# Row maximum as one rounded value, two steps' products together, reciprocals spread by four DMAs from SyncE: windowed attention and a ternary layer on one Trainium2 core

## The chip, the core and the metric

The kernel runs on one core of one Trainium2 chip. The time is device time in microseconds (us) from start to end of one execution. TensorE (PE) multiplies matrices, VectorE (DVE), ScalarE (ACT) and GpSimd (POOL) work element by element, SyncE (SP) issues most transfers between SBUF and DRAM. A median of three runs is given for the kernel before; the profile is of one execution of its own.

## The reference

`x` is 2048 tokens by 512, float32.

```python
qkv = layernorm(x) @ Wqkv                      # 512 -> 3 * 512
q, k = rope(rmsnorm(q, q_norm_w)), rope(rmsnorm(k, k_norm_w))   # 16 heads of 32
scores = q @ k.T / sqrt(32)                    # token i sees i-255 .. i
x = x + (softmax(scores) @ v) @ Wo
w_q = ternary(weight, 0.2, 0.6) + rram_variation
x = x + ternary(layernorm(x), 0.33, 0.5) @ w_q.T
```

## The kernel before, in words

**Three stages.** Up to about 188 us the inputs are normalised, projected, rotated and split: a float32 value is kept as a high part in TensorE's rounded form (float32r) and a low part, so that products of the three pieces high/high, high/low and low/high come near to float32. The pieces of q and k go to `qk_scr` in DRAM (L310). From about 188 to 463 us attention runs head by head. Then come the output projection (L703) and the ternary layer (L731).

**Attention** has 16 heads of 8 steps, `STEPS` = 128. A step has two tiles of 128 queries. All engines walk the same step numbers, each in a program of its own:

- TensorE, `scores` (L593), for step s: queries against three tiles of keys, into one of two pairs of PSUM banks. The left operand is a slice of `q_stack`, 128 rows: 96 of the three pieces, and 32 below them. Rows 96 and 97 of `q_stack` hold zeros at this time, and rows 96 and 97 of `k_stack` ones; the rest is zeros.
- VectorE, `merge` (L1169) and `maximum` (L1183): the largest masked score of each query, negated, in `neg_max`. `scores` of step s waits for the maximum of step s-2.
- After each fourth step `split_maxima` (L1192, L1194) splits eight columns of `neg_max` into high and low, TensorE transposes them to 16 rows (L601), VectorE copies them out (L1201), and SyncE writes them by DMA into rows 96 and 97 of `q_stack` (L418). This is step `M_TR` = 4c + 5 for half head c.
- TensorE, `scores_t` (L622), ten steps later (`ST_LAG`): the transposed scores S^T of the same step, keys against queries. The rows 96 and 97 now subtract the maximum. Its target `BANK_ST + e` is one bank for each of the two tiles; the tile's next S^T waits until ScalarE has read it (`expd`).
- ScalarE, `exponentials` (L849), two for each step, into `prob`; GpSimd zeroes what the window excludes (L1010, L1014).
- TensorE, `times_v` (L658): a half of the products of probabilities with `v` and with ones at each step, in 32-column tiles of the array. Each float32 matmul there shows as two in the trace.
- ScalarE copies results to `o_stage` (L859), SyncE stores them to `o_t` and the sums to `sum_scr` (L443, L447).

**Reciprocals.** A unit u is half of the tokens of four heads; there are eight. When its sums are in DRAM, they are loaded (`sums`), inverted on VectorE (L1237), stored (`rec_scr`), and spread over the 32 rows of each head into `rec_bc`; VectorE then divides `o_t` (L1244), two operations a unit. `after` gives the step at which a unit is complete. The tables `LOAD_SUMS`, `RECIP`, `STORE_RECS`, `SPREAD` and `DIVIDE` give the step of each. For u = 0 to 5 ScalarE issues the three transfers (L875, L881, L889), for the last two SyncE (L393, L399, L407). Steps go on to `LAST` = 160.

**SyncE's program** does at step s, in this order: the maxima's rows, the loads of the stacks of later heads (L368, at s % 8 of 6 and 2), staged results, spreads. A wait there holds all that stands behind it.

## Time and profile before

| | us |
|---|---|
| median of 3 runs | 561.16 (555.36 to 561.59) |
| the profiled execution | 562.22 |
| its span, first to last instruction | 560.3 |
| TensorE busy | 477.7 (85%) |
| VectorE busy | 382.6 (68%) |
| ScalarE busy | 212.1 (38%) |
| GpSimd busy | 226.4 (40%) |
| mean granted TensorE clock | 0.939 of 2.4 GHz |

Busy time is the time in which an engine had an instruction under way. Matmuls are pipelined and their ends are modelled, so a busy TensorE is not one at its peak. The chain of work that ended last is followed back from the end: 47% of the span on it is TensorE, 23% are transfers, 13% VectorE. The span less the busy time of an engine says nothing about where that engine was waited for.

### The profile page before, as it was taken

The page shows a single profiled execution, that of the slowest core. Times are in us where ns is not written, and L with a number is a line of the kernel's source. Part 1 is how long each engine was busy: PE and PEld are TensorE (multiplying, and loading weights), DVE is VectorE, ACT ScalarE, POOL GpSimd, SP SyncE. Part 2 cuts the span into 40 slices and gives each one's busy share as a digit, 9 for nine tenths or more (in the row PEclk, how much of TensorE's full clock was granted, in tenths as well). Part 3 has the DMA queues.
Part 4 walks back from the last instruction along what each step waited for, and adds up shares of the span by engine and source line. Part 5 has one row for each costly group of instructions (what it writes and reads, how often), then busy time and mean ns, then how long its engine had stood idle before and what let it go on. Part 6 is the DMA issues. An engine that isn't in the chain of part 4 may idle for free.

```text
span 560.3 us, 10469 instructions
## 1 busy us (share of the span) xinstructions
PE 477.7 (85%) x3648; PEld 338.8 (60%) x3648; DVE 382.6 (68%) x808; ACT 212.1 (38%) x464; POOL 226.4 (40%) x351
## 2 busy tenths in 40 slices
PE   1897997997997518797997799988997998788997
PEld 1685886786885305454664466555664656666775
DVE  3798478578377718484885888776775710798994
ACT  2451332233133114353554355534554471322121
POOL 2175288288297013242443244333443372423000
PEclk9998999999999858798999799988999799798999
DMA  8520466553548569766566455654454104302433
GB/s 289 202 77 0 168 207 227 176 173 143 187 152 216 199 181 235 256 170 159 142 179 165 117 168 142 183 150 113 138 143 122 50 23 127 99 23 75 135 110 132
DMA packets 42776, 83.41 MB, mean 149 GB/s; under 512 B 6803, under 2 KB 13747, under 8 KB 42471
## 3 DMA queue, kind: packets, MB, share of 16 engines
q1 hardware_dynamic: 40205, 79.40, 46.5%
q10 hardware_dynamic: 2520, 3.34, 2.1%
q8 instruction: 30, 0.49, 0.4%
q14 instruction: 21, 0.17, 0.1%
HBM read 48.12 MB, written 30.15 MB: 140 GB/s over the span
## 4 chain that ended last, share of the span: by engine, by line
PE 47%; DMA 23%; DVE 13%; POOL 6%; issue 5%; SPq 3%; ACT 2%; DVEq 0%; ACTq 0%; POOLq 0%
PE psum L658 12%; PE psum L622 9%; DMA rec_bc<-rec_scr 8%; DMA region_w<-max_rows 6%; PE psum L525 6%; PE psum L593 5%; PE psum L731 5%; PE psum L511 4%; PE psum L703 3%; DMA rec_scr<-recs 2%; SPq L310 2%; DMA qk_scr<-region_t 2%; POOL normed L983 2%; DVE region_o L1076 2%; DMA region_m<-in_x 2%
## 5 line engine op out<-in xcount | busy, mean ns | idle before, releaser
L849 ACT ACTIVATE region_m<-psum 128x384 f32<-128x384 f32 (+2 forms) x256 | 106.5, 468 | 134.9 <-PE psum L622 122.5
L1010 POOL TENSOR_SCALAR_AFFINE_SELECT region_m<-region_m 128x256 f32<-128x256 f32 x128 | 52.1, 407 | 167.0 <-ACT region_m L849 166.7
L658 PE MATMUL psum<-region_m,v 128*32 128x128 f32 (+1 forms) x992 | 113.8, 339 | 0.0
L658 PE MATMUL psum<-region_m,ones 128*32 128x128 f32 (+1 forms) x992 | 113.7, 338 | 0.0
L593 PE MATMUL psum<-region_w 128*128 128x384 f32 (+2 forms) x256 | 70.8, 362 | 29.4 <-DMA region_w<-qk_scr 15.7
L511 PE MATMUL psum<-region_t,region_w 128*128 128x512 f32 x384 | 93.6, 401 | 1.4 <-ACT region_t L763 1.4
L1169 DVE COPY_PREDICATED psum<-mask,psum 128x256 f32<-128x256 uint32 x128 | 54.5, 425 | 54.3 <-PE psum L593 38.9
L622 PE MATMUL psum<-region_w 128*128 128x384 f32 (+2 forms) x256 | 80.5, 397 | 12.7 <-DMA region_w<-max_rows 11.5
L511 PEld LDWEIGHTS psum<-region_t,region_w 128*128 128x128 f32 x384 | 72.5, 191 | 18.1 <-ACT region_t L763 1.8
L1183 DVE TENSOR_REDUCE neg_max<-psum 128x2 f32<-128x512 f32 x112 | 76.6, 684 | 2.5
L658 PEld LDWEIGHTS psum<-region_m,v 128*32 128x32 f32 x992 | 52.0, 112 | 42.6 <-issue 25.7
L622 PEld LDWEIGHTS psum<-region_w 128*128 128x128 f32 x256 | 40.9, 198 | 54.5 <-issue 41.2
L593 PEld LDWEIGHTS psum<-region_w 128*128 128x128 f32 x256 | 49.0, 207 | 33.3 <-DMA region_w<-qk_scr 14.1
L1076 DVE SCALAR_TENSOR_TENSOR region_o<-psum,qkw,region_m 128x512 f32<-128x512 f32 x64 | 43.6, 742 | 29.7 <-ACT region_o L774 29.7
L703 PE MATMUL psum<-region_t,region_w 128*128 128x512 f32 x192 | 48.5, 408 | 5.4 <-DVE region_w L1283 5.4
L658 PEld LDWEIGHTS psum<-region_m,ones 128*32 128x32 f32 x992 | 52.0, 112 | 0.0
L525 PE MATMUL psum<-region_w,region_t 128*128 128x512 f32 x192 | 49.2, 412 | 0.0
L703 PEld LDWEIGHTS psum<-region_t,region_w 128*128 128x128 f32 x192 | 37.8, 198 | 14.3 <-ACT region_w L868 5.8
L1014 POOL TENSOR_SCALAR_AFFINE_SELECT region_m<-region_m 128x256 f32<-128x256 f32 x112 | 45.5, 406 | 0.0
L525 PEld LDWEIGHTS psum<-region_w,region_t 128*128 128x128 f32 x192 | 36.8, 193 | 10.2 <-issue 2.7
L731 PE MATMUL psum<-region_t,region_w 128*128 128x512 f32 x128 | 34.5, 415 | 4.7 <-DVE normed L1325 4.7
L983 POOL TENSOR_TENSOR normed<-normed,half_h 128x512 fp32r<-128x512 f32 x26 | 33.5, 1312 | 11.6 <-ACT half_h L795 11.6
(88 smaller groups left out, 548.0 us busy)
## 6 DMA issues: line engine op xcount, KB each, us to landing
region_w<-qk_scr SPq DMA_DIRECT2D x60, 384.0 KB, 4.9
qk_scr<-half_h SPq DMA_DIRECT2D x56, 256.0 KB
region_m<-in_x SPq DMA_DIRECT2D x32, 256.0 KB, 3.4
qk_scr<-normed SPq DMA_DIRECT2D x28, 256.0 KB
region_o<-normed SPq DMA_DIRECT2D x64, 64.0 KB
out<-normed SPq DMA_DIRECT2D x16, 256.0 KB, 2.0
rec_bc<-rec_scr ACTq DMA_DIRECT2D x6, 512.0 KB
qk_scr<-region_t SPq DMA_DIRECT2D x8, 256.0 KB
```

The costliest lines, as they stand in the source:

```text
L511: last = nc.tensor.matmul(psum[:, BANK_PAIR + 2 * (n % 2) + half, :], w, x_t[g % 2][:, b, k, :], start=(k == 0 and a + b == 0), stop=(k == ...
L525: last = nc.tensor.matmul(psum[:, BANK_PAIR + 2 * (n % 2) + e, :], x_t[g % 2][:, b, k, P * i:P * (i + 1)], wv[:, a, k, :], start=(j == 0), ...
L593: last = nc.tensor.matmul(psum[:, 2 * (n % 2) + e, P * (k0 - qt + 2):3 * P], qs[:, P * qt:P * (qt + 1)], ks[:, P * k0:P * (qt + 1)], start ...
L622: last = nc.tensor.matmul(psum[:, BANK_ST + e, 0:P * (q1 - kt)], ks[:, P * kt:P * (kt + 1)], qs[:, P * kt:P * q1], start=True, stop=True)
L658: last = nc.tensor.matmul(psum[32 * r:32 * r + 32, BANK_O + c % 2, at:at + P * width], w, probs, start=start, stop=stop, tile_position=(0, ...
L703: last = nc.tensor.matmul(psum[:, BANK_WO + t % NWO, :], o_split[g % 2][:, a, c, P * i:P * (i + 1)], wo[:, b, c, :], start=(c == 0 and a + ...
L731: last = nc.tensor.matmul(psum[:, BANK_FFN + t % 2, :], xq_t[t % 2][:, c, :], wf[:, a, c, :], start=(j == 0), stop=(j == 7))
L849: nc.scalar.activation(prob[:, n % NPT, e, 0:cols], psum[:, BANK_ST + e, 0:cols], ACT.Exp, scale=SCALE).then_inc(expd, 1)
L1010: nc.gpsimd.affine_select(out=near, in_=near, compare_op=ALU.is_ge, fill=0.0, base=0, pattern=[[0, 2], [1, P]], channel_multiplier=-1).the ...
L1076: vec.scalar_tensor_tensor(rope[:, i, :], psum[:, banks + half, :], qkw[:, 2 * p + half:2 * p + half + 1], trig[:, g % 2, s, :], ALU.mult, ...
L1169: vec.copy_predicated(psum[:, 2 * (n % 2):2 * (n % 2) + 2, 0:P], mask[:, :, :].bitcast(U32), psum[:, 2 * (n % 2):2 * (n % 2) + 2, 2 * P:3 ...
L1183: vec.tensor_reduce(neg_max[:, h % 2, 2 * j:2 * j + 2], psum[:, slot:slot + 2, 0:2 * P], axis=AX_X, op=ALU.max, negate=True).then_inc(maxe ...
```

## The change

**Row maximum.** `tensor_reduce` now writes `neg_max` in float32r, so the value is rounded once, and the transpose takes it as it is: no `split_maxima`, 8 rows instead of 16, one row of the stack (96) instead of two. A rounded maximum is as good a shift as an exact one, since numerator and sum use the same.

**No zero rows.** `scores` contracts over 96 rows and `scores_t` over 97. The 32 rows of zeros and ones, their staging in DRAM, their loads for three stacks and the zeroing of two rows for each later head are gone; what is left is one row of ones for each of three stacks.

**Products of two steps together**, and another order of S^T and scores in every second step.

**Reciprocals.** All transfers of all units are issued by SyncE; one DMA for each head spreads 32 rows; the steps of the tables are earlier for units 0 to 5.

```diff
-        LOAD_SUMS = {n + (3 if u in BY_ACT else 2): u for u, n in after.items()}
-        RECIP = {n + (6 if u in BY_ACT else 5 + 2 * (u % 2)): u for u, n in after.items()}
-        STORE_RECS = {n + (8 if u in BY_ACT else 5 + 2 * (u % 2)): u for u, n in after.items()}
-        SPREAD = {n + (10 if u in BY_ACT else 7 + 2 * (u % 2)): u for u, n in after.items()}
-        DIVIDE = {n + (14 if u in BY_ACT else 10 + 3 * (u % 2)) + 2 * q: 2 * u + q
-                  for u, n in after.items() for q in range(2)}
+        LOAD_SUMS = {n + 3 - u % 2: u for u, n in after.items()}
+        RECIP = {n + 5 - u % 2: u for u, n in after.items()}
+        STORE_RECS = {n + 6 - u % 2: u for u, n in after.items()}
+        SPREAD = {n + 8 - u % 2: u for u, n in after.items()}
+        DIVIDE = {n + 11 - u % 2 + 2 * q: 2 * u + q for u, n in after.items() for q in range(2)}
...
-            eng.wait_ge(zero_set, 1)
-            rest = P - STACKED
-            eng.dma_start(zero_scr, rec_bc[0:rest, :]).then_inc(a_zero, 16)
-            eng.dma_start(ones_scr[MAXROWS:rest, :], rec_bc[0:rest - MAXROWS, :]).then_inc(a_zero, 16)
             eng.wait_ge(const_set, 4)
...
-                eng.dma_start(f32(q_stack[i][STACKED:P, :]), zero_scr).then_inc(a_ones[i], 16)
-                eng.dma_start(f32(k_stack[i][STACKED:P, :]), ones_scr).then_inc(a_ones[i], 16)
+                eng.dma_start(f32(k_stack[i][STACKED:STACKED + 1, :]), ones_scr).then_inc(a_ones[i], 16)
...
-                    eng.dma_start(f32(q_stack[i][STACKED:STACKED + MAXROWS, cols]),
-                                                        zero_scr[0:MAXROWS, cols]).then_inc(a_zeros[i][half], 16)
...
+                if s in LOAD_SUMS:
...
+                if s in STORE_RECS:
...
+                if s in SPREAD:
+                    u = SPREAD[s]
+                    c, half = divmod(u, 2)
+                    eng.wait_ge(a_recs[half], 16 * (c + 1))
+                    if c:
+                        eng.wait_ge(o_done, 2 * (u - 2) + 2)
+                    for h in range(4):
+                        eng.dma_start(
+                            rec_bc[HEAD_DIM * h:HEAD_DIM * (h + 1), 1024 * half:1024 * (half + 1)],
+                            rec_scr[half, 4 * c + h:4 * c + h + 1, :].to_broadcast(
+                                [HEAD_DIM, SEQ // 2])).then_inc(a_bc[half], 16)
...
             for s in range(STEPS + PV_LAG + 1):
-                if 0 <= s - ST_LAG < STEPS:
+                n = s - PV_LAG
+                if n % 2 and 0 <= s - ST_LAG < STEPS:
                     scores_t(s - ST_LAG)
                 if s < STEPS:
                     scores(s)
...
-                n = s - PV_LAG
-                if n > 0:
-                    times_v(n - 1 + n % 2, 1 - n % 2)
+                if n % 2 == 0 and 0 <= s - ST_LAG < STEPS:
+                    scores_t(s - ST_LAG)
+                if n > 0 and n % 2 == 0:
+                    for part in range(2):
+                        times_v(n - 1, part)
```

**TensorE in a quiet part of attention**, before. L622 is S^T, L593 the scores, L658 one half of the products; `x2` means two such instructions in a row.

```order
L622 MATMUL psum<-region_w 128x384 x2
L593 MATMUL psum<-region_w 128x384 x2
L658 MATMUL psum<-region_m,v 32x256
L658 MATMUL psum<-region_m,ones 32x256
L658 MATMUL psum<-region_m,v 32x256
L658 MATMUL psum<-region_m,ones 32x256
L658 MATMUL psum<-region_m,v 32x128
L658 MATMUL psum<-region_m,ones 32x128
L658 MATMUL psum<-region_m,v 32x128
L658 MATMUL psum<-region_m,ones 32x128
L622 MATMUL psum<-region_w 128x384 x2
```

And the same place now (L602 is S^T, L572 the scores, L638 the products):

```order
L602 MATMUL psum<-region_w 128x384 x2
L572 MATMUL psum<-region_w 128x384 x4
L602 MATMUL psum<-region_w 128x384 x2
L638 MATMUL psum<-region_m,v 32x256
L638 MATMUL psum<-region_m,ones 32x256
L638 MATMUL psum<-region_m,v 32x256
L638 MATMUL psum<-region_m,ones 32x256
L638 MATMUL psum<-region_m,v 32x128
L638 MATMUL psum<-region_m,ones 32x128
L638 MATMUL psum<-region_m,v 32x128
L638 MATMUL psum<-region_m,ones 32x128
```

The scores of two steps now stand in one run between two S^T, and both halves of the products (sixteen rows, of which eight are shown) follow the second S^T.

**SyncE around the first unit**, steps 45 to 49, before. L418 writes the maxima's rows, L368 loads a stack, L443 and L447 store staged results; the transfers of the reciprocals stand in ScalarE's program.

```order
L418 DMA region_w<-max_rows 2x8x128
L365 DMA region_w<-zero_scr 2x1024
L368 DMA region_w<-qk_scr 96x1024 x2
L443 DMA sum_scr<-normed 2x2x256
L447 DMA region_o<-normed 32x2x256 x2
L418 DMA region_w<-max_rows 2x8x128
```

And now, the same steps (L380, L354, L405, L409 for the same transfers; L422 stores reciprocals, L416 loads the next unit's sums, L431 spreads):

```order
L380 DMA region_w<-max_rows 1x8x128
L354 DMA region_w<-qk_scr 96x1024 x2
L422 DMA rec_scr<-recs 128x32
L405 DMA sum_scr<-normed 2x2x256
L409 DMA region_o<-normed 32x2x256 x2
L416 DMA sums<-sum_scr 128x32
L431 DMA rec_bc<-rec_scr 32x1024 x4
L380 DMA region_w<-max_rows 1x8x128
```

Between the rows of step 45 and those of step 49 there are now one store, one load and four spreads more, and one zeroing less.

## Rows read from the trace of the kernel before

**Rows 1.** Stretches, matmuls of L622 alone: length, PE, PEld busy (count), PEclk, DMA share, GB/s.

```profile
260.00:290.00 30.00, 10.60 (x36) 5.36 (x36) 1.00 0.53 145
290.00:322.00 32.00, 8.46 (x28) 4.32 (x28) 0.89 0.57 152
352.00:388.00 36.00, 10.43 (x32) 5.26 (x32) 0.91 0.58 157
418.00:443.00 25.00, 7.38 (x22) 3.69 (x22) 0.86 0.35 95
```

**Rows 2.** The chain of waits near 290 us: start, length, what.

```profile
290.27 3.99 DMA rec_scr<-recs
294.28 14.47 DMA rec_bc<-rec_scr
```

**Rows 3.** Stretches of 2 us, all engines; the last two columns are DMA share, GB/s.

```profile
194.00:196.00 2.00, 0.00 (x0) 0.00 (x0) 2.00 (x6) 0.08 (x1) 0.00 (x0) 0.50 0.52 203
474.00:476.00 2.00, 0.00 (x0) 0.00 (x0) 0.00 (x0) 0.00 (x0) 0.00 (x0) 1.00 0.26 99
```

**Rows 4.** The timeline of one step: start, length, engine, line, what, idle before.

```profile
286.16 0.44 PE L622 MATMUL psum<-region_w 128*128 128x384 f32 x1
286.44 0.33 PE L622 MATMUL psum<-region_w 128*128 128x384 f32 x1
286.61 0.34 PE L593 MATMUL psum<-region_w 128*128 128x384 f32 x1
286.70 0.87 ACT L849 ACTIVATE region_m<-psum 128x384 f32<-128x384 f32 x2 [0.92 <-PE psum L622]
287.05 0.40 PE L658 MATMUL psum<-region_m,v 128*32 128x256 f32 x1
287.16 0.43 DVE L1169 COPY_PREDICATED psum<-mask,psum 128x256 f32<-128x256 uint32 x1 [0.21 <-PE psum L593]
287.62 0.69 DVE L1183 TENSOR_REDUCE neg_max<-psum 128x2 f32<-128x512 f32 x1
287.84 0.62 PE L622 MATMUL psum<-region_w 128*128 128x384 f32 x2
```

**Rows 5.** Timeline and chain after the last scores, where steps have S^T and products only.

```profile
452.84 0.62 PE L622 MATMUL psum<-region_w 128*128 128x384 f32 x2
454.18 0.62 PE L622 MATMUL psum<-region_w 128*128 128x384 f32 x2
461.44 2.13 PE psum L658 x48
```

**Rows 6.** The chain before and in the first heads, and a stretch as in rows 3.

```profile
192.17 10.82 DMA qk_scr<-region_t
219.43 10.87 DMA region_w<-max_rows
218.00:230.00 12.00, 8.31 (x98) 4.79 (x96) 6.97 (x18) 4.55 (x11) 3.47 (x9) 0.96 0.87 237
```

**Rows 7.** The chain at the end of attention.

```profile
466.65 1.68 DMA rec_scr<-recs
468.35 8.79 DMA rec_bc<-rec_scr
479.37 1.63 PE psum L703 x3
```

**Rows 8.** The timeline of SyncE in step 46 and of TensorE at the end of attention.

```profile
288.86 1.82 SPq L368 DMA_DIRECT2D region_w<-qk_scr  x2
479.37 9.06 PE L703 MATMUL psum<-region_t,region_w 128*128 128x512 f32 x27 [5.42 <-DVE region_w L1283]
```

**Rows 9.** The timeline of VectorE at the second group of inputs.

```profile
21.21 2.47 DVE L1042 BATCH_NORM_STATS2 stats<-region_m 128x6 f32<-128x512 f32 x4 [2.53 <-DMA region_m<-in_x]
```

**Rows 10.** Groups by line and shape: busy us, mean ns, idle before.

```profile
L1228 DVE TENSOR_SCALAR region_t<-psum 128x128 fp32r<-128x128 f32 x16 | 4.5, 282 | 0.0
```

**Rows 11.** The tile `rec_scr`, all its eight stores.

```profile
DMA to landing us min/median/max: 1.4/4.7/9.4
```

More of the change, by code:

```diff
@@ L43 @@
 STACKED = 3 * HEAD_DIM
-MAXROWS = 2
 NSTACK = 3
@@ L143, in build @@
         NWO = 5
-        zero_set, a_zero = steps("zero_set"), steps("a_zero")
+        a_one = steps("a_one")
         const_set, mask_set, ident_cast = steps("const_set"), steps("mask_set"), steps("ident_cast")
@@ L165, in build @@
         a_ones = [steps(f"a_ones{i}") for i in range(NSTACK)]
-        a_zeros = [[steps(f"a_zeros{i}{half}") for half in range(2)] for i in range(NSTACK)]
         a_rows = [steps(f"a_rows{i}") for i in range(2)]
@@ L447, in _ @@
                         eng.dma_start(dst[:, e], src).then_inc(a_stage[c % 2], 16)
-                if s in SPREAD and SPREAD[s] not in BY_ACT:
-                    spread_recs(SPREAD[s])
-                if s in LOAD_SUMS and LOAD_SUMS[s] not in BY_ACT:
-                    load_sums(LOAD_SUMS[s])
-                if s in STORE_RECS and STORE_RECS[s] not in BY_ACT:
-                    store_recs(STORE_RECS[s])
+                if s in LOAD_SUMS:
+                    u = LOAD_SUMS[s]
+                    c, half = divmod(u, 2)
+                    eng.wait_ge(a_stage[half], 48 * (4 * c + 4))
+                    if u - 2 >= 0:
+                        eng.wait_ge(recd, u - 1)
+                    eng.dma_start(sums[:, u % 2, :], sum_scr[half, 4 * c:4 * c + 4, :].rearrange(
+                        "h (i t) -> (h i) t", t=32)).then_inc(a_sums[u % 2], 16)
+                if s in STORE_RECS:
+                    u = STORE_RECS[s]
+                    c, half = divmod(u, 2)
+                    eng.wait_ge(recd, u + 1)
+                    eng.dma_start(rec_scr[half, 4 * c:4 * c + 4, :].rearrange("h (i t) -> (h i) t", t=32),
+                                  recs[:, half, :]).then_inc(a_recs[half], 16)
+                if s in SPREAD:
+                    u = SPREAD[s]
+                    c, half = divmod(u, 2)
+                    eng.wait_ge(a_recs[half], 16 * (c + 1))
[6 more added lines that the diff above has]
+                                [HEAD_DIM, SEQ // 2])).then_inc(a_bc[half], 16)
                 if s in (STEPS + PV_LAG + 2, STEPS + PV_LAG + 4):
@@ L593, in scores @@
                     last = nc.tensor.matmul(psum[:, 2 * (n % 2) + e, P * (k0 - qt + 2):3 * P],
-                                            qs[:, P * qt:P * (qt + 1)],
-                                            ks[:, P * k0:P * (qt + 1)], start=True, stop=True)
+                                            qs[0:STACKED, P * qt:P * (qt + 1)],
+                                            ks[0:STACKED, P * k0:P * (qt + 1)], start=True, stop=True)
                 last.then_inc(score, 1)
             def maxima_to_rows(c, s):
-                eng.wait_ge(m_low, c + 1)
-                nc.tensor.transpose(psum[0:2 * PAIRS, 2 * (s % 2), 3 * P:4 * P],
-                                              f32(max_split[:, c % 2, :]), ident[:, :]).then_inc(m_tr, 1)
+                h, half = divmod(c, 2)
+                eng.wait_ge(maxed, 4 * c + 4)
+                nc.tensor.transpose(psum[0:PAIRS, 2 * (s % 2), 3 * P:4 * P],
+                                    f32(neg_max[:, h % 2, PAIRS * half:PAIRS * (half + 1)]), ident[:, :]).then_inc(m_tr, 1)
             def transpose_w(i):
@@ L947, in _ @@
             nc.gpsimd.memset(mask[:, :, :], 1.0).then_inc(const_set, 1)
-            nc.gpsimd.memset(rec_bc[:, :], 0.0).then_inc(zero_set, 1)
             eng.wait_ge(const_set, 4)
@@ L1023, in _ @@
                     for half in range(2):
-                        eng.wait_ge(a_bc[half], 16 * CHUNKS)
+                        eng.wait_ge(a_bc[half], 64 * CHUNKS)
                     for i in (2, 3):
@@ L1175, in maximum @@
                 eng.wait_ge(merged, n + 1)
-                if h >= 2:
-                    eng.wait_ge(m_low, 2 * (h - 2) + j // 4 + 1)
+                if h >= 2 and j % 4 == 0:
+                    eng.wait_ge(m_tr, 2 * (h - 2) + j // 4 + 1)
                 if j == 0:
```

90 lines of the change are left out of this document (12 added, 78 removed).

## The prediction

> **What bounds the kernel now.** I read the page's totals, then the matmuls of one line counted stretch by stretch, then the chain of waits at the places where the count falls, then single steps. The totals are a mean over stages that have different limits, so nothing below rests on them. The profiled execution took 562.2 us, 0.2% over the median of 561.2; the sum below is made against 562.2. The change touches attention (about 188 to 479 us) and little else.
>
> In attention every step issues two matmuls of L622, so their count gives the pace. 260 to 290 us has 36 of them: 18 steps, 1.667 us each; two more stretches of 30 us (322 to 352, 388 to 418) have 36 too. The three between them, in which reciprocals are spread, have 28, 32 and 22, that is 14, 16 and 11 steps, which should take 23.3, 26.7 and 18.3 us and take 32, 36 and 25 [rows 1]. They lose 8.7 + 9.3 + 6.7 = 24.7 us, part of it at the half clock (granted 0.89, 0.91 and 0.86 against 1.00).
>
> The chain of waits names the loser: `rec_bc<-rec_scr` takes 14.47 us from issue to landing [rows 2], and VectorE, which has the division next in its program, can't go on to the maxima. On an idle core it takes 8.79 us too [rows 7]. Why so long: while it is alone in flight, the share of the DMA engines is 0.26 at 99 GB/s, four engines of sixteen at 25 GB/s; the `qk_scr` stores, whose outermost size is 8, show 0.52 at 203 GB/s [rows 3]. The old access pattern has 4 heads outermost. The Trainium skill, DMA: Bandwidth & Descriptors, in "Why a DMA increments its semaphore by 16 and not by 1", says that a DMA uses the largest count up to 16 that divides the outermost sizes of both sides: 4 before, 16 for a new piece of 32 rows; the trace agrees as far as it goes (0.26 and 0.52).
>
> **The spread: engines.** A new piece is 128 KB over 32 rows. 
> **The spread: order.** The cover changes, since sums, reciprocals and spreads now stand in SyncE's one program and queue, and DIVIDE comes 11 steps after the units' table entry `after` instead of 14. First unit: SyncE issues the stack load of step 46 at 288.86 for 1.82 us [rows 8]; the store of the reciprocals goes behind it, 290.7; it takes 3.99 as before [rows 2], 294.7; four spreads are issued until 297.1 and land by 299.1. VectorE comes to the division of step 51 at 296.6 (step 46 starts at 286.16 [rows 4], five steps of 1.667, and 2.15 until the maximum ends). It waits 2.5 us. TensorE feels it only at scores two steps on, about 1 us. Meanwhile the row maxima of step 49, behind the spreads in SyncE's program, go out at 297.1 instead of 293.4 and land at 299.2; S^T of step 53 wants them at 298.3: 0.9, mostly the same wait. I take 1.5 us for a unit, 3 for a stretch of two, 9 for all three; no half clock. Gain 24.7 − 9 = **15.7 us** (bounds 0 and 24.7). ScalarE no longer stands in these waits, which TensorE felt little.
>
> **Zero rows.** Four fills of 256 KB go before the last stores, and two in front of the third stack. The last store is issued at 192.17 and lands 10.82 us later [rows 6], with eight engines full at 25.4 GB/s each [rows 3]; 1 MB over 16 engines is 65.5 KB on each of them: **2.6 us** less before the loads that TensorE waits for. The row maxima issued at 219.43 wait 10.87 us behind a backlog that moves 237 GB/s [rows 6]; 0.5 MB less is **2.1 us** (bounds 0 and 4.7 for both). At the start 0.5 MB goes from before `load_x(1)`, for which VectorE idles 2.53 us [rows 9]; its next consumer, the squares, waits for matmuls until 25 us anyway: 0.4 (0 to 1.3). The small zero loads of each head are 8 KB: nothing. The contraction goes from 128 rows to 96 and 97; no row here has fewer than 128. The spacing of 0.17 us is 0.01 over the 384 columns at 2.4 GHz, so 512 matmuls could give 5 us at most; I take 0.
>
> **Row maximum.** The two small VectorE operations for each half head go, 64 in all; VectorE is not what TensorE waits for in a quiet stretch, so 0. The transpose waits for `maxed` 4c+4, which the scores ahead of it have waited for already.
>
> **Products together.** Two steps were S^T, S, PV, S^T, S, PV; now S^T, S, S, S^T, PV, PV. From the row times [rows 4]: the first S^T matmul starts at 0, the second at 0.28, the scores at 0.45, the product at 0.89, the next S^T at 1.68. Within one kind the spacing is 0.17, so a junction costs about 0.11 before S^T's second matmul, 0.10 between scores and product, and 0.12 after products (48 matmul pieces, three parts, in 2.13 against 3 × 0.79 [rows 5]). A pair of steps saves 0.33 of 3.36. But the bank of S^T is single: the second S^T waits for the exponentials of the first. They start 0.54 after it and end at 1.41 [rows 4]. In the new order the second matmul of the second S^T would load at 1.13; it must wait until 1.45. That gives back 0.32: **0 us** for 59 pairs (bounds: −19.5 without that wait; +3.5 if the release of the bank takes 0.1 and not 0.04). VectorE now gets two scores 0.34 apart. Its merge starts 0.55 after the scores and merge and maximum take 1.15 [rows 4], so the later maximum ends at 3.35; the scores that want it start at 3.35 + 0.79 = 4.14. The slack of 0.8 holds a division (0.7) but not the splitting of a ternary weight (four operations of 0.28 [rows 10]): 8 × 0.3 = **+2.4**. After step 128 there are no scores to stand between two S^T: the second S^T starts 1.18 after the first (the first exponential ends at 0.97, release 0.04, load 0.17), its second matmul at 1.62, products at 1.89 for 1.46: 3.35 against 2 × 1.34 [rows 5]; 5 pairs, **+3.3**.
>
> **The tail.** TensorE idles 5.42 us before L703, to 479.37 [rows 8], on the last spread but one (468.35, 8.79) [rows 7]. In the new program the store of its reciprocals goes after two x loads (about 0.9 after the 466.65 of before), lands beside them about 470, the pieces are out at 472.5 and land at 474.5: **−2.7**, and **−0.8** for the half clock after the idle (three matmuls in 1.63 us [rows 7], half of that at the full one). Bounds −1 and −6. The last unit comes 10 us earlier, but its division on GpSimd is hidden before and after.
>
> Sum: 562.2 − 15.7 − 4.7 − 0.4 + 2.4 + 3.3 − 3.5 = **543.6 us**.
>
> **Rivals.**
> (a) *S^T does not wait*: the exponentials start earlier than I read, and the junctions count in full, 59 × 0.33 = 19.5: 524 us. For it: TensorE is fully busy in quiet stretches, no exponential being waited for. Against: the 1.41 is a row. Chance 0.15.
> (b) *Four pieces are no faster*: they read the same rows again and again, and a spread still lands 8.8 us after its issue, now later by 1.8 and with SyncE behind it. The stretches keep their 24.7: 562.2 − 4.7 − 0.4 + 5.7 − 1 = 562 us. The Trainium skill, DMA: Bandwidth & Descriptors, "Rules for kernel authors", says of transfers to disjoint partition halves "Don't bother — they serialize", and wants one of 128 partitions; that holds for pieces that already use all engines, which the 0.26 says this one does not. Chance 0.12.
> (c) *Stalls of 3 us for each unit* because VectorE has lost its slack: 9 more: 553 us. Chance 0.12.
> (d) *SyncE holds the row maxima* (the slower side): in its program they stand behind the wait for the reciprocals' landing. It decides when a unit costs more than 4.1 us (24.7 / 6). With the longest landing of reciprocals, 9.4 us [rows 11], instead of 3.99, the row maxima go out at 302.5 and come 6 us late for S^T, and the half clock after it costs 1.7 (0.11 of 32 us, for two units [rows 1]): 7.7 × 6 = 46, less the 9 that I have, is 37 over my sum, 581 us. For it: a stack load is ahead in the same queue. Against: 3.99 was measured beside the same load. Chance 0.05.
> The forecast, 535 to 552 us, has 0.56.
>
> **Numbers.** 543.6 us is that of the likeliest. With (a) and (c) inside, 524 to 555 leaves (b), (d) and a little out: 8 in 10. A difference of 2% is what a measurement can tell here, so faster means under 549.9: forecast almost whole (0.50), (a) 0.15, and a part of (c) 0.04: 0.69. Within 2%: 0.24, mostly (b) and (c). Slower: 0.07, (d) and what I don't see.
>
> **What would show it.** Landing of `rec_bc` pieces within 5 us of the first issue, and a share near 1 while they fly; the three stretches at 1.8 us a step with a granted clock near 1; TensorE's S^T waiting for ScalarE's exponentials some 0.3 us in each pair (about 18 us in the table of waits), else (a); VectorE waiting for `rec_bc` under 10 us instead of 24.6 in sum; the idle before the first last-chunk projection near 3 us; the first row-maximum waits shorter. Wrong it would be if the queue of SyncE makes reciprocals land late.

## The result, and the profile after

The changed kernel takes **540.1 us** (median of 4 runs, 536.9 to 546.0) against 560.7 us of the kernel before (4 runs, 555.4 to 561.6) on the same chip: a ratio of 0.963, 95% interval 0.955 to 0.972. The forecast was 543.6 us in a range of 524 to 555. Some executions of every kernel take some per cent longer at a lower granted clock: medians are of all runs, and ratios compare the others alone. The changed kernel's profiled execution took 536.9 us with a span of 534.1; the one of before, 562.2 with a span of 560.3. The two traces so differ by 26.2 us where the medians differ by 20.6: the profiled execution after is the quickest of its kernel's runs, and the one before lies 1.5 us above its median.

I cut both traces at the same work: the issue of the row maxima of the seventh half head (257.8 before, 250.2 after), that of the last half head (451.4 and 421.4), the last product of attention (463.5 and 436.5), and the restart of TensorE in the output projection (479.4 and 450.7).

| stretch | before | after | change | forecast |
|---|---|---|---|---|
| to the seventh row maxima | 257.8 | 250.2 | −7.6 | −5.1 |
| 100 steps to the last row maxima | 193.6 | 171.2 | −22.4 | −13.3 |
| to the last product | 12.1 | 15.1 | +3.0 | +3.3 |
| to the projection's restart | 15.9 | 14.2 | −1.7 | −2.7 |
| to the end | 80.9 | 83.4 | +2.5 | −0.8 |

The matmuls of S^T (now L602) by stretches, which answer to [rows 1]: start and end, length, PE, PEld busy (count), PEclk, DMA share, GB/s.

```profile
258.00:288.00 30.00, 11.10 (x36) 5.88 (x36) 1.00 0.61 172
288.00:318.00 30.00, 9.85 (x34) 5.43 (x34) 1.00 0.66 179
318.00:348.00 30.00, 10.16 (x32) 5.66 (x33) 0.94 0.61 164
380.00:410.00 30.00, 10.80 (x34) 5.59 (x34) 1.00 0.51 142
```

A stretch with spreads now holds 32 to 36 matmuls in 30 us, where there were 28 in 32 and 22 in 25, and the clock is nearly whole. In the 100 steps TensorE was at its half clock for 22.5 us before and for 3.4 after.

The DMA issues of SyncE in the after trace, one unit of reciprocals (start, length, queue, line, what), then the page's row for all 32 pieces (KB each, median us to landing), then who waited (total, times, longest).

```profile
283.31 1.71 SPq L431 DMA_DIRECT2D rec_bc<-rec_scr  x4
285.07 0.72 SPq L380 DMA_DIRECT2D region_w<-max_rows  x1
```

```profile
rec_bc<-rec_scr SPq DMA_DIRECT2D x32, 128.0 KB, 2.7
```

```profile
DVE region_o L1185 <- DMA rec_bc<-rec_scr: 8.7, 5, 2.7
PE psum L602 <- ACT region_m L832: 7.4, 7, 4.1
PE psum L602 <- DMA region_w<-max_rows: 3.3, 4, 1.5
```

One wait is new. SyncE's program waits for the landing of the reciprocals' store before it issues the spreads, and the next row maxima stand behind them. The wait in the whole run (total, times, longest), and two pieces of the chain of waits near 340 us (start, length, what):

```profile
SPq L431 <- DMA rec_scr<-recs: 6.4, 7, 2.3
```

```profile
334.12 5.10 DMA rec_scr<-recs
341.00 2.25 DMA region_w<-max_rows
```

Here SyncE issues nothing from 338.1 to 339.24, then the four spreads, then the row maxima, and S^T starts when these have landed.

The four pieces of this unit are issued within 1.7 us and the last lands at 287.3, 4.0 us after the first issue, for 14.47 in [rows 2]; each piece posts 16 semaphore updates when it lands, where the old DMA posted 5. VectorE waits 8.7 us for reciprocals in all, for 24.6 before.

### The profile page after: what moved, and what is told of

The parts are those of the page before. It is cut to its first block, busy times and chain, and to the rows that moved or that the text cites. A ratio compares the mean times of both kernels' runs of the same rounds, so it can differ in the third digit from the quotient of the medians.

```text
span 534.1 us, 10283 instructions
## 1 busy us (share of the span) xinstructions
PE 465.0 (87%) x3648; PEld 345.1 (65%) x3648; DVE 369.4 (69%) x744; ACT 210.5 (39%) x464; POOL 226.3 (42%) x350
## 4 chain that ended last, share of the span: by engine, by line
PE 49%; DVE 17%; DMA 10%; SPq 8%; issue 7%; POOL 4%; ACT 3%; DVEq 0%; ACTq 0%; POOLq 0%
PE psum L638 11%; PE psum L602 8%; PE psum L506 8%; PE psum L492 5%; PE psum L714 5%; PE psum L572 5%; PE psum L686 4%; DMA rec_scr<-recs 3%; DVE region_o L1028 3%; SPq L409 2%; DMA region_w<-max_rows 2%; DMA rec_bc<-rec_scr 2%; PE psum L527 2%; DVE diag L1040 2%; SPq L354 1%
## 5 line engine op out<-in xcount | busy, mean ns | idle before, releaser
L962 POOL TENSOR_SCALAR_AFFINE_SELECT region_m<-region_m 128x256 f32<-128x256 f32 x128 | 54.3, 424 | 141.4 <-ACT region_m L832 141.4
L638 PE MATMUL psum<-region_m,ones 128*32 128x128 f32 (+1 forms) x992 | 98.9, 330 | 0.0
L638 PE MATMUL psum<-region_m,v 128*32 128x128 f32 (+1 forms) x992 | 98.9, 330 | 0.0
L602 PE MATMUL psum<-region_w 97*128 97x384 f32 (+2 forms) x256 | 81.7, 394 | 10.6 <-ACT region_m L832 7.4
L572 PE MATMUL psum<-region_w 96*128 96x384 f32 (+2 forms) x256 | 66.4, 367 | 19.9 <-DMA region_w<-qk_scr 13.3
L1135 DVE TENSOR_REDUCE neg_max<-psum 128x2 fp32r<-128x512 f32 x112 | 76.6, 684 | 2.5
L602 PEld LDWEIGHTS psum<-region_w 97*128 97x128 f32 x256 | 44.0, 196 | 50.2 <-issue 33.6
L638 PEld LDWEIGHTS psum<-region_m,v 128*32 128x32 f32 x992 | 57.8, 111 | 20.7 <-issue 7.8
L572 PEld LDWEIGHTS psum<-region_w 96*128 96x128 f32 x256 | 45.7, 203 | 29.3 <-DVE neg_max L1135 13.1
L638 PEld LDWEIGHTS psum<-region_m,ones 128*32 128x32 f32 x992 | 57.8, 111 | 0.0
L966 POOL TENSOR_SCALAR_AFFINE_SELECT region_m<-region_m 128x256 f32<-128x256 f32 x112 | 45.9, 409 | 0.0
```

Source lines behind the costliest of these rows:

```text
L572: last = nc.tensor.matmul(psum[:, 2 * (n % 2) + e, P * (k0 - qt + 2):3 * P], qs[0:STACKED, P * qt:P * (qt + 1)], ks[0:STACKED, P * k0:P * ...
L602: last = nc.tensor.matmul(psum[:, BANK_ST + e, 0:P * (q1 - kt)], ks[0:STACKED + 1, P * kt:P * (kt + 1)], qs[0:STACKED + 1, P * kt:P * q1], ...
L638: last = nc.tensor.matmul(psum[32 * r:32 * r + 32, BANK_O + c % 2, at:at + P * width], w, probs, start=start, stop=stop, tile_position=(0, ...
L962: nc.gpsimd.affine_select(out=near, in_=near, compare_op=ALU.is_ge, fill=0.0, base=0, pattern=[[0, 2], [1, P]], channel_multiplier=-1).the ...
L1135: vec.tensor_reduce(neg_max[:, h % 2, 2 * j:2 * j + 2], psum[:, slot:slot + 2, 0:2 * P], axis=AX_X, op=ALU.max, negate=True).then_inc(maxe ...
```

## The experiments

Times are medians, with the ratio to the kernel before on the same chip and its 95% interval.

**1. One spread for each unit.**

```diff
-                    for h in range(4):
-                        eng.dma_start(
-                            rec_bc[HEAD_DIM * h:HEAD_DIM * (h + 1), 1024 * half:1024 * (half + 1)],
-                            rec_scr[half, 4 * c + h:4 * c + h + 1, :].to_broadcast(
-                                [HEAD_DIM, SEQ // 2])).then_inc(a_bc[half], 16)
+                    eng.dma_start(
+                        rec_bc[:, 1024 * half:1024 * (half + 1)],
+                        rec_scr[half, 4 * c:4 * c + 4, :].rearrange("h (o t) -> h o t", o=1).to_broadcast(
+                            [4, HEAD_DIM, SEQ // 2])).then_inc(a_bc[half], 16)
```

(In this kernel and the next the two waits on `a_bc` count 16 and 32 for a unit.)

> The changed kernel with the reciprocals of a unit spread by one DMA instead of four (same queue, same steps, same bytes). Theory E (DMA engines): one DMA over four heads is carried by few of the 16 engines, as in the kernel before, so it lands 9 to 14 us after its issue instead of 4, the divisions wait for it, the VectorE queue holds the row maxima behind them, and most of the 18 us that the stretches with spreads gained is lost: 552 to 560 us, with waits of VectorE for rec_bc of over 20 us in sum. Rival P (place): what helped is that SyncE issues the chain and issues it earlier; then the time stays at 538 to 543 us.

Measured: **574.1 us**, 1.020 (1.010 to 1.030). Theory E has the direction and is short by 14 us at least: this is slower than the kernel before. The profiled executions here (581.0 us) and in experiment 7 (569.5) are above their medians, so sums of waits read in them may be a few us too large.

**2. Two spreads of two heads.**

```diff
-                    for h in range(4):
+                    for h in (0, 2):
                         eng.dma_start(
-                            rec_bc[HEAD_DIM * h:HEAD_DIM * (h + 1), 1024 * half:1024 * (half + 1)],
-                            rec_scr[half, 4 * c + h:4 * c + h + 1, :].to_broadcast(
-                                [HEAD_DIM, SEQ // 2])).then_inc(a_bc[half], 16)
+                            rec_bc[HEAD_DIM * h:HEAD_DIM * (h + 2), 1024 * half:1024 * (half + 1)],
+                            rec_scr[half, 4 * c + h:4 * c + h + 2, :].rearrange("h (o t) -> h o t", o=1).to_broadcast(
+                                [2, HEAD_DIM, SEQ // 2])).then_inc(a_bc[half], 16)
```

> The changed kernel with a unit's reciprocals spread by two DMAs of two heads each. Theory E: the outermost dimension of a DMA (2 here) sets how many engines carry it, so each is carried by 2 of the 16 and both land no sooner than the single DMA of four heads does: 555 to 570 us, landing 9 to 18 us after the first issue. Rival N (number of pieces): more DMAs in flight are quicker whatever their shape; then it lies between the changed kernel and the one with a single spread, about 546 us.

Measured: **614.0 us**, 1.095 (1.087 to 1.102), slower by 40 us than with one spread and 44 above the range expected: theory E has the direction again, and what one more slow DMA costs it had far too low. The number of pieces is not what helps; each piece's shape is. Stretches of 1.5 and 4 us in which no engine works and a spread is what the DMA engines carry (PE, PEld, DVE, ACT, POOL busy, PEclk, DMA share, GB/s), first of experiment 1:

```profile
299.50:301.00 1.50, 0.00 (x0) 0.00 (x0) 0.00 (x0) 0.00 (x0) 0.00 (x0) 0.50 0.25 72
```

and of experiment 2:

```profile
301.00:305.00 4.00, 0.00 (x0) 0.00 (x0) 0.00 (x0) 0.00 (x0) 0.00 (x0) 0.50 0.13 52
```

A DMA of four heads keeps a quarter of the 16 DMA engines busy, one of two heads an eighth, and both sorts post that number of semaphore updates and one more (5 and 3). In experiment 2 the first piece's last two updates come at 300.15 and 301.01 and those of the second, issued 0.6 us behind it, at 305.14 and 306.00, 4.99 us after each; the share is 0.12 (299 to 300) while both are in flight. So they stand on the same two engines, one behind the other. The Trainium skill, DMA: Bandwidth & Descriptors, in "Why a DMA increments its semaphore by 16 and not by 1", says that a DMA issued from SyncE or ScalarE runs on the lowest-numbered engines. The trace does not number them; that both pieces share their two agrees.

**3. TensorE's order of before in the changed kernel.**

```diff
-                n = s - PV_LAG
-                if n % 2 and 0 <= s - ST_LAG < STEPS:
+                if 0 <= s - ST_LAG < STEPS:
                     scores_t(s - ST_LAG)
...
-                if n % 2 == 0 and 0 <= s - ST_LAG < STEPS:
-                    scores_t(s - ST_LAG)
-                if n > 0 and n % 2 == 0:
-                    for part in range(2):
-                        times_v(n - 1, part)
+                n = s - PV_LAG
+                if n > 0:
+                    times_v(n - 1 + n % 2, 1 - n % 2)
```

> The changed kernel with TensorE's order of before: S^T first in every step, one half of the products in every step. My account from the traces: a quiet pair of steps 3.28 -> 3.36 us (+4 us over some 50 pairs), the end phase behind the last score 3.1 us shorter, so 541 us (538 to 544). Rival: putting the products of two steps together is worth its nominal 0.3 us in each of 59 pairs; then 555 to 558 us.

Measured: **540.2 us**, 0.961 (0.952 to 0.969), inside the range expected: the products together are worth nothing as a whole that the medians can tell. By the trace the 100 steps take 177.3 us for 171.2 (with 7.6 us at the half clock for 3.4), and the stretch from the last row maxima to the last product 12.1 for 15.1; the rest of the difference lies ahead of attention's steady part, where kernels with the same front differ by up to 9 us in my traces (247.6 to 256.9 at the seventh row maxima).

**4. Four spreads in the kernel before.** The edit is that of experiment 1 backwards, in both functions `spread_recs`, with 64 for 16 in the waits on `a_bc`.

```diff
-                eng.dma_start(
-                    rec_bc[:, 1024 * half:1024 * (half + 1)],
-                    rec_scr[half, 4 * c:4 * c + 4, :].rearrange("h (o t) -> h o t", o=1).to_broadcast(
-                        [4, HEAD_DIM, SEQ // 2])).then_inc(a_bc[u % 2], 16)
+                for h in range(4):
+                    eng.dma_start(
+                        rec_bc[HEAD_DIM * h:HEAD_DIM * (h + 1), 1024 * half:1024 * (half + 1)],
+                        rec_scr[half, 4 * c + h:4 * c + h + 1, :].to_broadcast(
+                            [HEAD_DIM, SEQ // 2])).then_inc(a_bc[u % 2], 16)
```

> The kernel before with only the spread cut into four DMAs, of one head each, still issued by ScalarE at its old steps. Theory E: they land 4 us after the first issue, the 18 us in the stretches with spreads come back less the time that ScalarE takes to issue three more (its exponentials stand behind them, 3 x 0.4 us in each of 6 units, hidden or not): 543 to 550 us. Rival P: the place counts; then 556 to 561 us.

Measured: **545.5 us**, 0.975 (0.966 to 0.984), 14 us from this edit alone (9 to 19 by the interval), inside the range expected; the 100 steps take 175.8 us for 193.6. Which engine issues the chain, and at which step, shows no gain beside it: with SyncE's places, TensorE's old order and no zero rows (experiment 3) they take 177.3, one trace each.

**5. The row maximum and the zero rows, alone and apart.** Two kernels: the kernel before with the hunks of the diff on `MAXROWS`, `zero_scr`, `neg_max`, `max_split` and the row counts of the matmuls; and the same with the split into two values kept.

```diff
-                eng.dma_start(f32(q_stack[i][STACKED:P, :]), zero_scr).then_inc(a_ones[i], 16)
-                eng.dma_start(f32(k_stack[i][STACKED:P, :]), ones_scr).then_inc(a_ones[i], 16)
+                eng.dma_start(f32(k_stack[i][STACKED:STACKED + MAXROWS, :]), ones_scr).then_inc(a_ones[i], 16)
...
-                    eng.dma_start(f32(q_stack[i][STACKED:STACKED + MAXROWS, cols]),
-                                                        zero_scr[0:MAXROWS, cols]).then_inc(a_zeros[i][half], 16)
```

Expected of the first:

> The kernel before with only the row maxima changed: one value in TensorE's rounded form, 97 rows in S^T, no rows of zeros, ones written once; spreads and the order of TensorE as before. My account (front): the row-maximum DMA of the seventh half head is issued 7.6 us earlier in the changed kernel, nearly all of it from these parts, and the steps gain 1 to 3 us more because the row-maximum DMA now takes twice as many DMA engines and VectorE has no splitting: 548 to 553 us against 559. Rival: the front gain is a matter of the runs' start (the load of x); then 555 to 559 us.

Of the second:

> The kernel before with the rows of zeros and the fills for them gone, but the row maximum still split into two values (98 rows in S^T). The prediction put 4.7 us on the zero rows and nothing on the row maximum; the run with both came out 9.2 us faster. If the zero rows carry it all: 549 to 553 us. If the split and its two-row DMA were worth about half: 554 to 557 us.

Measured: the first **0.984** (0.978 to 0.989), about 551 us for 560.4 by the ratio (the median of all ten runs is 556.6); the second 553.7 us, **0.983** (0.974 to 0.992). The zero rows carry it all, 9 us (6 to 12 by the narrower interval), and the single row maximum nothing that can be told. In the trace of the second the seventh row maxima go out at 250.0 us (257.8 before) and the 100 steps take 191.9 for 193.6. A single trace is not enough for the first of these: the seventh row maxima go out at 257.7 to 262.9 us in the three traces of kernels with zero rows and at 247.6 to 256.9 in the eleven without, 6.8 us apart in the mean. The row maxima's DMA runs on four times the DMA engines and not on twice: it posts 9 updates for 3.

**6. Exponentials over 128 columns, after and before.** The same edit in both kernels.

```diff
-                    nc.scalar.activation(prob[:, n % NPT, e, 0:cols], psum[:, BANK_ST + e, 0:cols],
+                    nc.scalar.activation(prob[:, n % NPT, e, 0:P], psum[:, BANK_ST + e, 0:P],
```

> The changed kernel with each exponential over 128 columns instead of up to 384: two thirds of the exponentials' work is left out, so the output is not the reference's. Theory B (bank): in a quiet pair of steps the second S^T waits for the first exponentials to free its bank, and this is what held the pair at 3.28 us where its instructions need 3.03; then the pair falls to 3.0 to 3.1 us and the 100 steps between the seventh and the last row-maximum DMA take 158 to 163 us instead of 171. Rival I (issue): TensorE is bound by its own weight loads and issue; the pair stays at 3.25 to 3.3 us and the 100 steps at 168 to 172.

> The control: the kernel before with the same shorter exponentials (their other columns left out of the work). There S^T opens every step and waits for nothing in quiet steps, so by both theories its quiet pair stays at 3.36 us and its 100 steps at 188 to 196 us.

Measured, one run each: 528.5 us in the changed kernel, 563.8 in the one before. A quiet pair is two steps in which TensorE waits for no row maxima and no maximum. One in the timeline of TensorE (start, length, line, what), of the changed kernel:

```profile
268.41 0.61 PE L602 MATMUL psum<-region_w 97*128 97x384 f32 x2
268.86 0.98 PE L572 MATMUL psum<-region_w 96*128 96x384 f32 x4
269.67 0.64 PE L602 MATMUL psum<-region_w 97*128 97x384 f32 x2
271.68 0.61 PE L602 MATMUL psum<-region_w 97*128 97x384 f32 x2
```

its exponentials:

```profile
268.94 0.87 ACT L832 ACTIVATE region_m<-psum 128x384 f32<-128x384 f32 x2 [1.35 <-PE psum L602]
270.11 0.88 ACT L832 ACTIVATE region_m<-psum 128x384 f32<-128x384 f32 x2 [0.29 <-PE psum L602]
```

and with short exponentials, TensorE and then ScalarE:

```profile
267.25 0.62 PE L602 MATMUL psum<-region_w 97*128 97x384 f32 x2
267.71 0.86 PE L572 MATMUL psum<-region_w 96*128 96x384 f32 x4
268.41 0.51 PE L602 MATMUL psum<-region_w 97*128 97x384 f32 x2
270.29 0.62 PE L602 MATMUL psum<-region_w 97*128 97x384 f32 x2
```

```profile
267.79 0.45 ACT L832 ACTIVATE region_m<-psum 128x128 f32<-128x128 f32 x2 [1.42 <-PE psum L602]
```

The second S^T starts 1.26 us after the first beside whole exponentials and 1.16 beside short ones, its two matmuls are 0.64 and 0.51 us long, and the pair takes 3.27 and 3.04 us. Of the 55 pairs behind the first eight, the lower quarter goes from 3.26 to 3.03 us and the median from 3.28 to 3.23; what holds the other half near 3.2 stays open. In the kernel before the lower quarter stays at 3.37 and the 100 steps take 188.4, as expected. Theory B holds for the quiet pair and is too large for the whole: the 100 steps fall to 165.8 us, not to 158 to 163.

**7. One spread, with the divisions three steps later.** Why is experiment 1 slower than the kernel before, which has the same DMA? On top of its edit:

```diff
-        DIVIDE = {n + 11 - u % 2 + 2 * q: 2 * u + q for u, n in after.items() for q in range(2)}
+        DIVIDE = {n + (14 if u < 6 else 11) - u % 2 + 2 * q: 2 * u + q for u, n in after.items() for q in range(2)}
```

> The single spread per unit again, with the divisions of the first six units three steps later (14 steps behind the unit's end instead of 11). If the cost of the slow spread is that VectorE waits for it in its queue with the row maxima behind, six steps (9.7 us at 1.62 us each) between issue and division cover nearly all of a landing of 9 to 11 us: 541 to 548 us, against 574 with the early divisions. Rival: the long transfer itself disturbs (DMA engines, row-maximum DMAs, clock) wherever the division stands; then 555 us or more.

Measured: **566.6 us**, 1.004 (0.999 to 1.009). The rival is right in the main. In the steps VectorE no longer waits for `rec_bc` (29.3 us in experiment 1), and that gave only 7.5 us by the medians (574.1 to 566.6). The chain of waits of this kernel (start, length, what):

```profile
294.02 0.61 SPq L430
294.63 0.04 issue
294.67 9.04 DMA region_w<-max_rows
303.71 0.04 issue
303.76 1.01 PE psum L601 x2
```

The row maxima, 4 KB, are issued behind the spread and land at 303.71; the spread has landed at 303.53. This is a second path from the slow spread to TensorE, past VectorE: the maxima of this kernel take 9.0, 9.5 and 9.1 us behind the three first spreads, those of experiment 1 11.1, 9.2 and 10.3, those of experiment 2 14.1, 13.8 and 15.0, and 1.8 to 2.5 in the steps where no spread is ahead. Their updates show the place: of the eight that come with the landing, four of experiment 1 come 2.0 us after the issue (292.39 to 292.47) and four behind the spread's four (301.25 to 301.49 behind 301.07 to 301.31); in experiment 2 six come by 293.9 and two at 305.3 and 306.2, behind 305.1 and 306.0. Only what shares the spread's DMA engines is late. In the steps S^T waits for them three times, 19.4 us in sum here and 22.5 in experiment 1. In the kernel before it is there too, across queues: ScalarE's spread of [rows 2] lands at 308.75, and the maxima that SyncE issued at 300.71 land at 308.78. There, though, the spread was ten steps behind its unit and met the row maxima late in its flight; on SyncE, two steps earlier, they go out 0.65 us behind it and wait for nearly all of it.

**8. Both ends mended.** From step 128 on the old order of TensorE, and the loads of `x` behind the last spreads.

```diff
                 n = s - PV_LAG
-                if n % 2 and 0 <= s - ST_LAG < STEPS:
+                paired = s < STEPS
+                if (n % 2 or not paired) and 0 <= s - ST_LAG < STEPS:
...
+                if not paired:
+                    times_v(n - 1 + n % 2, 1 - n % 2)
...
-                if s in (STEPS + PV_LAG + 2, STEPS + PV_LAG + 4):
+                if s in (STEPS + PV_LAG + 6, STEPS + PV_LAG + 10):
```

> The changed kernel with two things mended at the end: behind the last score (step 128 on) TensorE goes back to S^T first and half the products in each step, and SyncE issues the four loads of x behind the stores and spreads of the last reciprocals instead of ahead of them. By the comparison of the traces the first gives 3.1 us (5.8 by the run of the alternating order) and the second 3 us on the chain from the last staging to the projection: 532 to 536 us against 540 of the changed kernel. Rival: the loads of x then come late for the first residual additions and the second gives nothing: 535 to 538 us.

Measured: **531.6 us** (6 runs, 525.8 to 537.5), 0.946 (0.941 to 0.951): faster than both kernels, and 0.4 us below the range expected. From the last row maxima to the last product it takes 12.1 us for 15.1, from there to the projection's restart 11.2 for 14.2. The chain at that place, first of the changed kernel:

```profile
440.15 3.88 DMA rec_scr<-recs
444.05 0.33 SPq L431
```

and of this one, where the store (issued at 433.39) lands in 2.10 us, before SyncE has issued what the last half head wants, and the chain goes by the spread:

```profile
437.07 2.77 DMA rec_bc<-rec_scr
439.84 0.02 issue
439.87 0.70 DVE region_o L1188
```

**9. Short subtractions on GpSimd, on top of 8.** What makes the stretch behind the restart longer than before?

```diff
+                n = GROUP if g == 0 else 32
-                nc.gpsimd.tensor_tensor(o_split[g % 2][:, 1, c, :], o_t[:, c, GROUP * g:GROUP * (g + 1)],
+                nc.gpsimd.tensor_tensor(o_split[g % 2][:, 1, c, 0:n], o_t[:, c, GROUP * g:GROUP * g + n],
```

> The version with both ends mended, and the late subtractions of GpSimd (the low halves of the output's splits, all but those of the first four hundred and more tokens) over 32 columns instead of 512; the rest of these halves is left out. Theory: VectorE's tensor_scalar over 128x512 takes 1.15 and 1.40 us beside these subtractions and 0.56 and 0.43 us alone; with them short all four such operations of the first two tiles fall to 0.4 to 0.7 us and the stretch from the projection's restart to the end from 82.0 to 79 to 80.5 us. Rival: these operations are slow for a reason of their own (first use, the half clock); then they keep their 1.1 to 1.4 us.

Measured, one run: 530.1 us. VectorE and then GpSimd in the changed kernel:

```profile
455.57 0.55 DVE L1250 TENSOR_SCALAR v<-v,mean_var,rstd 128x512 f32<-128x512 f32 x1
456.15 1.40 DVE L1253 TENSOR_SCALAR v<-v 128x512 bf16<-128x512 f32 x1
457.58 1.66 DVE L1257 SCALAR_TENSOR_TENSOR v<-v 128x512 bf16<-128x512 f32 x1
459.16 0.68 DVE L1234 TENSOR_TENSOR v<-psum,region_m 128x512 f32<-128x512 f32 x1
```

```profile
455.86 4.52 POOL L952 TENSOR_TENSOR region_w<-region_o,region_w 128x512 fp32r<-128x512 f32 x3 [4.13 <-ACT region_w L851]
```

In experiment 8 the same two TENSOR_SCALAR of the first tile take 1.15 and 1.40 us and the first of the second 1.17; here

```profile
454.21 0.63 DVE L1254 TENSOR_SCALAR v<-v,mean_var,rstd 128x512 f32<-128x512 f32 x1
454.88 0.49 DVE L1257 TENSOR_SCALAR v<-v 128x512 bf16<-128x512 f32 x1
455.40 1.66 DVE L1261 SCALAR_TENSOR_TENSOR v<-v 128x512 bf16<-128x512 f32 x1
```

with the last of them still beside GpSimd's multiplication (455.04 to 458.2). From the projection's restart to the end it is 78.4 us, for 82.0 in experiment 8: a little more than the 1.5 to 3 us expected. VectorE is busy for 62.8 us of it for 66.6, and 3.4 us of it are at the half clock for 6.8, which one run cannot take apart. The Trainium skill, SBUF — State Buffer, "SBUF: two separate sides", has VectorE and GpSimd share a pair of ports, which one of them holds for a whole instruction where VectorE's has two inputs in SBUF or runs in a mode that takes both its ports. The 1.40 beside 0.43 agrees, and so does the addition that reads PSUM, 0.68 beside the same subtractions and elsewhere.

**10. Divisions one step later, on top of 8.**

```diff
-        DIVIDE = {n + 11 - u % 2 + 2 * q: 2 * u + q for u, n in after.items() for q in range(2)}
+        DIVIDE = {n + (12 if u < 6 else 11) - u % 2 + 2 * q: 2 * u + q for u, n in after.items() for q in range(2)}
```

> The version with both ends mended, and the divisions of the first six units one step later. In it VectorE still waited 1 to 2.7 us for the spreads in a unit; with 1.6 us more between, 4 to 6 us of the 100 steps should go: 526 to 530 us against 531.6. If the stalls of the stretches with spreads come from the divisions' own time on VectorE (two times 0.7 us per unit and step) and not from the wait, 530 to 533 us.

Measured: **534.9 us**, 0.950 (0.944 to 0.956), above both ranges expected and no gain over experiment 8. VectorE's wait for `rec_bc` in the steps fell from 7.2 to 4.1 us, but the 100 steps of the trace take 177.3 us for 171.2, with 12.2 us at the half clock for none, 8.8 of them at their start. One pair, from 348.2 us, takes 7.1 us: the chain there goes by SyncE, which idles for 1.6 us until its store of the reciprocals has landed (5.61 us from 342.17) and whose row maxima, behind the spreads, land at 352.1; the half clock begins after this wait, at 352.9. Behind the pair a division (0.80) stands on VectorE between a ternary weight's operation and the merge of the next scores. Whether the later divisions bring this about, and whether it hides a gain, stays open.

## Why the prediction was right, and where not

**Spreads: right, size and cause of the landing.** Forecast −15.7; experiment 4 measures −14.0 (0.975; 9 to 19 by its interval), and −17.8 in the 100 steps of its trace, with the spreads in their old places on ScalarE. The landing I worked out as 4.5 us is 4.0, by 16 engines for each piece; experiments 1 and 2 exclude the rival cause, more DMAs in flight. What I had wrong is how a slow spread hurts. I let it act through VectorE alone; experiment 7 shows the path through the DMA engines, on which the row maxima sit behind the spread. It did not spoil the sum, because both paths end with the landing, and [rows 1] held both. It would have spoilt rival (b): with slow pieces on SyncE I gave 562 us, experiment 1 gives 574. Rival (d), SyncE holding the row maxima behind the wait for the reciprocals' landing, is there, in a small size: the landings on the chain are 4.4 to 5.1 us and not 9.4, SyncE idles for them 6.4 us in all, and TensorE waits 3.3 us for row maxima (11.5 before). With slow spreads the DMA engines hold the row maxima too, which no rival had.

**Zero rows: right sign, half the size.** Forecast −4.7; measured −9, 6 to 12 by the interval (experiment 5), above my bound of 4.7. Where it comes, the fourteen traces tell in part. The last store before the first heads lands 10.8 us after its issue in the three kernels with zero rows, as in [rows 6], and 6.6 to 7.3 in the eleven without: 3.8 us, where I had put 2.6. From there to the seventh row maxima it is 52.4 to 54.7 us with zero rows and 51.1 to 54.6 without, 1.0 apart in the mean, where I had put 2.1. The trace after also has that store's issue 3.2 us sooner (188.9 for 192.2), but kernels without zero rows issue it anywhere from 188.9 to 196.8, so this is no effect that can be told from the runs' own spread. What makes up the rest of the 9 is open.

**Row maximum: right**, 0 (experiment 5), also for the contraction: S^T's matmuls over 384 columns take 402 ns with 97 rows and 409 with 128, the scores 377 with 96 and 372 with 128: no gain.

**Products together: the mechanism right, the steps mis-sized.** The second S^T does wait for the exponentials of the first (experiment 6), and the ideal pair is the 3.03 that I named. The wait gives back 0.23 of the 0.33 and not 0.32, by the pair 3.36, 3.27 and 3.04; why less was not tested. The median pair takes 3.28 us for 3.39 in the old order of experiment 3: 0.1 in each of 50 pairs, some 5 us. The +2.4 for the ternary weights came too. In the 100 steps of the trace after TensorE's scores wait for VectorE's maximum (total, times, longest):

```profile
PE psum L572 <- DVE neg_max L1135: 3.8, 10, 0.7
```

All waits of over 0.1 us that stand right behind the splitting of a ternary weight are eight, 0.13 to 0.50 us long and 2.1 us in sum. In the two traces with the old order and fast spreads (experiments 3 and 4) there is none of them. So 3 of the 6.1 us between 177.3 and 171.2 are accounted for; the trace of experiment 3 has 4.2 us more at the half clock, which can stand for 2 at most, and the rest is open. At the end of the scores the order costs 3.0, as forecast (+3.3). Net 3 us are left by the traces; the medians of experiment 3 show 0, with some 5 us of uncertainty each.

**The tail: half.** Forecast −2.7 to the restart; measured −1.7, since the store of the reciprocals took 3.88 us beside the loads of `x` for which I gave it about 2.5 (experiment 8 takes these loads away and gets 2.9 us back). The −0.8 for the half clock did not come: the first three matmuls of the projection take 1.64 us for 1.63 before, and 0.95 in experiment 8, where the idle before them is 0.8 us for 3.7. Behind the restart it is +2.5, which I had not seen. GpSimd's late subtractions now fall on two tiles of VectorE's quantization where they fell on one; VectorE's 48 operations of it take 32.0 us for 31.1, so this is 0.9 of the 2.5. The rest is not shown: experiment 3, with the same program on SyncE, takes 80.9 us there, and the kernels with the old end 80.9 to 84.2.

**The sum.** I started from 562.2 us, where the median before is 560.7, so the change that I forecast is −18.6 us and the measured one −20.6. That they lie 2 us apart is in part luck, because the misses have both signs: 4 us too little for the zero rows and 8 for the order of TensorE (6 gained in the steps of one trace, where I had +2.4), against 2 too much for the spreads and 4 for the tail. Their net of 6 is more than the 2, by less than the uncertainty of one ratio. Rival (a), 524 us, is excluded by experiment 6: it would need the 3.03 in each pair.

**The signs.** The pieces land in 4.0 us (within 5), VectorE waits 8.7 us for them (under 10), and the stretches shown have 1.67 to 1.88 us a step (1.8). The share near 1 did not come (0.73 at 239 GB/s from 284.5 to 286.5), and the idle before the restart is 3.7 us (near 3). One sign failed and would have pointed to rival (a): the table of waits was to show some 18 us of S^T waiting for exponentials, and has 0.5 us of it in the 100 steps. It could not show them: the second S^T starts at 269.67, before the scores ahead of it end (268.86 + 0.98), so TensorE has no idle time there. Experiment 6 was needed to tell.

## What to carry to other kernels

Look at the outermost size of a DMA's access pattern before its bytes: a broadcast over 4 heads ran on 4 of 16 DMA engines, and four DMAs of 32 rows did the same 512 KB in 4 us instead of 8 to 14; two DMAs of two heads were worse than one of four. A slow DMA also delays small ones that somebody waits for, on other queues too, so compare their landings before you give an engine's wait for the cause. An engine that issues in the order of its program can hold small transfers as well, behind a landing that it waits for (here 6.4 us of such waits on SyncE). When one order pays in the steady part and costs where its partner work ends, switch at that point: here, by the traces, it was worth as much as the whole reordering.

## What was unexpected

- A transfer of 4 or 8 KB took 8 to 15 us, in the cases named above, while a spread on 2 or 4 DMA engines was in flight ahead of it, and landed 0.03 to 0.2 us behind it, from the same queue or another.
- Two spreads on 2 DMA engines each moved 45 to 52 GB/s, one behind the other, with the share of the 16 engines at 0.12 to 0.13.
- The reordering that was to save nothing saved 3 to 6 us in the steps by the traces and lost 3 at their end, and both could be kept apart by one condition on the step.
